# A four-layer attention network on one core: first keys and queries of the two split attentions made in other stages, and the last part of the network as one chunked stage

## What is computed

```python
x = x + _L0_xattn_ref(_layernorm(x), ctx_512, ...)
x = x + _L0_ffn_ref(_layernorm(x), ...)
...
x = x + _L2_ffn_ref(_layernorm(x), ...)
x = x + _L3_xattn_ref(_layernorm(x), ctx_512, ...)
x = x + _L3_ffn_ref(_layernorm(x), ...)

def fp4_quant_dequant(x):
    scale = jnp.maximum(jnp.max(jnp.abs(xb), -1, keepdims=True) / 6.0, 1e-12)
    idx = jnp.searchsorted(_MID, jnp.abs(xb / scale))
    return _GRID[idx] * jnp.sign(xb / scale) * scale
h = silu(fp4_linear(x, w_gate)) * fp4_linear(x, w_up)
return fp4_linear(h, w_down)
```

## Time and profile before

| | |
|---|---|
| median of 3 runs | 4032.26 us (4030.01 to 4044.68) |
| the profiled execution | 4038.64 us, span 4036.9 us |
| PE busy | 3242.3 us (80%) |
| DVE busy | 2389.7 us (59%) |
| ACT busy | 1805.8 us (45%) |
| POOL busy | 1094.5 us (27%) |
| mean granted TensorE clock | 0.905 of full speed |
| DMA | 89.94 MB, mean 22 GB/s |

### The profile page before, as it was taken

The page is one execution under the profiler, slowest core; times in us unless marked ns, Lnnn a source line. Parts: engine busy times, 40 slices in busy tenths (PEclk is TensorE's granted clock), DMA queues, the critical chain, the costliest instruction groups (busy, mean ns, idle before and its releaser), DMA issues. The chain is left out here.

```text
span 4036.9 us, 81036 instructions
## 1 busy us (share of the span) xinstructions
PE 3242.3 (80%) x33476; PEld 1634.2 (40%) x33476; DVE 2389.7 (59%) x3851; ACT 1805.8 (45%) x2194; POOL 1094.5 (27%) x767
## 2 busy tenths in 40 slices
PE   7985999999588827999999999977876799999821
PEld 5661333332266513444444444444542233333311
DVE  4554788878456454555555555433435688688676
ACT  2321677676333223444444444432211477677611
POOL 1002112110233253655565656631001111111000
PEclk9995999999799867999999999988877799899965
DMA  0003111110000030000000000001202211111000
GB/s 26 2 12 69 44 32 33 34 38 11 17 22 2 1 76 6 10 10 2 10 10 10 2 10 2 2 1 33 59 17 50 50 33 39 34 41 27 2 6 11
DMA packets 69858, 89.94 MB, mean 22 GB/s; under 512 B 37582, under 2 KB 50427, under 8 KB 69499
## 3 DMA queue, kind: packets, MB, share of 16 engines
q1 hardware_dynamic: 65642, 78.37, 8.6%
q10 hardware_dynamic: 3856, 6.47, 0.9%
HBM read 34.17 MB, written 4.33 MB: 10 GB/s over the span
## 5 line engine op out<-in xcount | busy, mean ns | idle before, releaser
L1970 DVE TENSOR_REDUCE mx<-ps 128x2 f32<-128x802 f32 (+1 forms) x1372 | 1028.2, 778 | 292.5 <-PE ps L1836 267.5
L1904 ACT ACTIVATE probs<-ps 128x1024 f32<-128x1024 f32 (+1 forms) x832 | 832.9, 1024 | 257.1 <-PE ps L1822 248.3
L2282 DVE TENSOR_REDUCE mx<-ps 128x3 f32<-128x1203 f32 (+1 forms) x352 | 483.1, 1373 | 476.7 <-PE ps L2178 476.7
L2330 POOL TENSOR_TENSOR sums<-sums,probs 128x2048 f32<-128x2048 f32 x128 | 579.1, 4524 | 143.7 <-ACT probs L2257 129.0
L1836 PE MATMUL ps<-kt,qs 48*128 48x401 bf16 x2048 | 472.4, 355 | 115.2 <-DVE mx L1970 79.0
L2257 ACT ACTIVATE probs<-ps 128x1024 f32<-128x1024 f32 x384 | 372.2, 1021 | 358.0 <-PE ps L2156 357.9
L1854 PE MATMUL ps<-probs,v_cur 128*9 128x256 f32 x6656 | 530.0, 391 | 0.4 <-ACT probs L1904 0.4
L2178 PE MATMUL ps<-kt,qt 32*128 32x401 f32 x2048 | 339.8, 556 | 46.4 <-DVE mx L2282 40.8
L1822 PE MATMUL ps<-qs,kt 50*128 50x256 bf16 (+1 forms) x3328 | 346.3, 281 | 1.8 <-ACT probs L1904 1.4
L2011 POOL CAST max_pieces<-negm 128x8 bf16<-128x8 f32 x64 | 12.1, 189 | 1122.2 <-DVE negm L1975 1122.2
L1836 PEld LDWEIGHTS ps<-kt,qs 48*128 48x128 bf16 x2048 | 134.6, 95 | 331.8 <-DVE mx L1970 255.6
(11 more groups left out here) (402 smaller groups left out, 4268.0 us busy)
## 6 DMA issues: line engine op xcount, KB each, us to landing
kt<-k SPq DMA_DIRECT2D x776, 50.0 KB
ctx_s<-in_ctx_t SPq DMA_DIRECT2D x16, 400.2 KB, 4.6
ctx_s<-ctx_norm_t SPq DMA_DIRECT2D x16, 400.2 KB, 5.5
qs<-q ACTq DMA_DIRECT2D x24, 192.0 KB
ctx_norm_t<-ctx_norm_t SPq DMA_DIRECT2D x8, 400.2 KB
ctx_a<-in_ctx_t SPq DMA_DIRECT2D x8, 400.2 KB
ctx_b<-in_ctx_t SPq DMA_DIRECT2D x8, 400.2 KB
ctx_tok<-in_ctx SPq DMA_DIRECT2D x8, 384.0 KB
```

Of the source, the lines that this page charges most:

```text
L1904: act.activation(pr[0:m, u % 3, :], pair[0:m].rearrange("p a n -> p (a n)"), ACT.Exp, scale=scale).then_inc(s_free, 1)
L1970: dve.tensor_reduce(mx[:, n % 2, i0:i0 + count], src, AX_X, ALU.max).then_inc(freed(step), 1)
L2282: dve.tensor_reduce(mx[:, n % 2, 3 * i0:3 * i0 + count], rbanks[:, 0:count, 0:CH], AX_X, ALU.max).then_inc(ring_free, 1)
L2330: pool.tensor_tensor(o, o, p, ALU.add).then_inc(added, 1)
```

## The change

Two things, in one edit.

**First keys and queries ready.** `SplitTiles` holds the buffers of `split_cross` outside of it, with `kt` as two tensors, `kt0` and `kt1`. `FirstKeys` makes the keys of batch 0 in earlier stages: in `layer0` inside `normalized` (loads, projection, drains) and in the new `first_queries` (pieces on POOL), which also holds the former `int4_lora` and projects and splits all queries of layer 0 on DVE; the 24 sends of keys and queries and five of the seven weight loads go into `self_heads`, whose SP issued nothing in `layer0`. For `layer3` the loads are in the `normalized` of the layer 2 FFN, and projection, drains, pieces and sends in `experts`. Layer 3's queries stay in `split_cross`: the first 512 are split by DVE and sent half by SP and half by ACT, the other 1536 are split by POOL after the first `cut` and sent by SP.

**One last stage.** `finish` replaces everything from the transpose of y to the store. It works in four chunks through PE, ACT, DVE and POOL, quantizes with a shorter chain, treats the three weights as one array of 1120 columns (loaded in layer 3's `normalized`, after a `clear`), and stores each chunk when it is done.

```diff
+class FirstKeys:
...
+    def fetch(self, sp):
+        for dst, src in self.loads:
+            sp.dma_start(dst, src).then_inc(self.ctx_in, 16)
...
+    def project(self, pe, k):
+
+        pe.wait_ge(self.ones_set, 1)
+        pe.wait_ge(self.ctx_in, 32)
+        for c, (lo, hi) in enumerate(CHUNKS):
+            pe.matmul(k.ps[:, 4 + c, 0:hi - lo], self.wk[0:R, :], self.tiles.ctx_s[0:R, 0, lo:hi], start=True,
+                      stop=True).then_inc(self.filled, 1)
...
+    def send(self, sp):
+        for i, (dst, src) in enumerate(self.tiles.key_sends()):
+            sp.wait_ge(self.cut, (1, 3, 4)[sorted(KPIECE)[i // 2]])
+            sp.dma_start(dst, src).then_inc(self.sent, 16)
+        sp.wait_ge(self.sent, 16 * 2 * PIECES)
...
+def first_queries(nc, k, keys, tiles, xt, wcq, bcq, y, w, at, b):
...
+        @block.tensor
+        def _(pe):
+            for c in range(4):
+                pe.matmul(k.ps[:, 4 + c, :], wcq, xt[:, cols4(c)], start=True, stop=True).then_inc(filled, 1)
+            pe.matmul(k.ps[:, 1, 0:C], at, b, start=True, stop=True).then_inc(lora, 1)
...
+            qp = tiles.qp
+            dve.wait_ge(drained, 4)
+            dve.tensor_copy(qp[0][:], qf).then_inc(cut, 1)
+            dve.wait_ge(cut, 1)
+            dve.tensor_tensor(qf, qf, qp[0][:], ALU.subtract).then_inc(cut, 1)
+            dve.wait_ge(cut, 2)
+            dve.tensor_copy(qp[1][:], qf).then_inc(cut, 1)
+            dve.wait_ge(cut, 3)
+            dve.tensor_tensor(qp[2][:], qf, qp[1][:], ALU.subtract).then_inc(cut, 1)
+
+        @block.gpsimd
+        def _(pool):
+            keys.pieces(pool)
...
-    slots = [(-80.0, ("qproj", 0))] + [(-70.0 + c, ("qproj", c)) for c in range(1, 4)]
-    steps = [(-90.0, ("ctx", 0)), (-90.0, ("ctx", 1)), (-89.0, ("ones",)), (-74.0, ("qsplit", 0)), (-73.9, ("qsend", 0)),
-             (-42.4, ("qsplit", 1)), (-42.3, ("qsend", 1))]
+    slots, steps = [], [(-90.0, ("ones",)), (-89.0, ("ctx", 1))]
+    if not ready:
+        slots += [(-80.0, ("qproj", 0))] + [(-71.0 + c, ("qproj", c)) for c in range(1, 4)]
+        steps += [(-69.9, ("qsplit", 0)), (-69.8, ("qsend", 0)), (3, ("qsplit", 1)), (25, ("qsend", 1))]
     for b in range(B):
...
-        slots += [(at - 22.5 + c, ("kproj", b, c)) for c in range(4)]
-        steps += [(at - 17 + 2.4 * i, ("ksplit", b, i)) for i in range(4)]
...
+        if b >= 1:
+            slots += [(at - 22.5 + c, ("kproj", b, c)) for c in range(4)]
+            steps += [(at - 17 + 2.4 * i, ("ksplit", b, i)) for i in range(4)]
...
+def fp4_round(dve, x, n, scales, a, e, step, base):
...
+    dve.tensor_reduce(rs, x, AX_X, ALU.max, apply_absolute_value=True).then_inc(step, 1)
...
+    dve.tensor_scalar(sc, rs, 1.0 / 6.0, 1e-12, ALU.mult, ALU.max).then_inc(step, 1)
...
+    dve.reciprocal(rs, sc).then_inc(step, 1)
...
+    dve.tensor_scalar(rs, rs, FRACTION, None, ALU.mult).then_inc(step, 1)
...
+    dve.tensor_tensor(by16(an), x, wide(rs), ALU.mult).then_inc(step, 1)
...
+    dve.tensor_scalar(en.bitcast(I32), an.bitcast(I32), POWER, None, ALU.bitwise_and).then_inc(step, 1)
...
+    dve.tensor_scalar(en, en, 1.0, TWO_BITS, ALU.max, ALU.mult).then_inc(step, 1)
...
+    dve.tensor_tensor(an, an, en, ALU.add).then_inc(step, 1)
...
+    dve.tensor_tensor(an, an, en, ALU.subtract).then_inc(step, 1)
+
+
+def fp4_scaled(pool, x, n, scales, a):
+    wide = scales[:, 0, 0:n].rearrange("p (n a) -> p n a", a=1).broadcast_to([P, n, 16])
+    return pool.tensor_tensor(x, by16(a[:, 0:16 * n]), wide, ALU.mult)
...
+    plan = [("y", 0), ("wo", 0), ("y", 1), ("wo", 1), ("w", 0), ("n", 0), ("gu", 0), ("y", 2), ("wo", 2), ("n", 1),
+            ("gu", 1), ("y", 3), ("wo", 3), ("h", 0), ("down", 0), ("n", 2), ("gu", 2), ("h", 1), ("down", 1), ("n", 3),
+            ("gu", 3), ("h", 2), ("down", 2), ("h", 3), ("down", 3)]
...
+        def _(sp):
+            for c in range(4):
+                sp.wait_ge(final, c + 1)
+                sp.dma_start(out[:, tiles4(c), :], k.x[:, tiles4(c), :]).then_inc(stored, 16)
...
+            def gate(c):
+                for t in range(NC * c, NC * c + NC):
+                    pool.wait_ge(silu_done, t + 1)
+                    pool.wait_ge(up_done, t + 1)
+                    pool.tensor_tensor(h[:, t, :], silu[:, t % 2, :], up[:, t % 2, :], ALU.mult).then_inc(gated, 1)
...
-def experts(nc, k, hid_t, w2, w):
+def experts(nc, k, hid_t, w2, w, keys):
...
             for t in range(NT):
+                if t == 2:
+                    keys.project(pe, k)
+                    pe.wait_ge(keys.drained, 4)
```

More of the change, by code:

```diff
@@ L191, in _ @@
         def _(sp):
+            if keys is not None:
+                keys.fetch(sp)
             if src_dram is not None:
@@ L217, in _ @@
         def _(pool):
+            if keys is not None:
+                keys.set_ones(pool)
             for c in range(4):
@@ L2001, in _ @@
                     split_queries(pool, 1)
-                elif kind == "ksplit" and step[1] >= 1:
+                elif kind == "ksplit":
                     split_keys(pool, step[1], step[2])
@@ new lines, in hidden, with last @@
+            def hidden(c):
+                dve.wait_ge(gated, NC * c + NC)
+                fp4("h", c)
+            def last(c):
+                dve.wait_ge(down_done, c + 1)
+                dve.tensor_tensor(k.x[:, tiles4(c), :], bank4(k.ps[:, 7, :]), k.x[:, tiles4(c), :], ALU.add).then_inc(final, 1)
+            fp4("w", 0)
+            add(0)
+            add(1)
+            norm(0)
+            norm(1)
+            add(2)
+            hidden(0)
+            norm(2)
+            add(3)
+            hidden(1)
@@ L2613, in experts, with _ @@
         block = ctx.enter_context(nc.Block())
+        @block.sync
+        def _(sp):
+            keys.send(sp)
+        @block.scalar
+        def _(act):
+            keys.drain(act, k)
+        @block.gpsimd
+        def _(pool):
+            keys.pieces(pool)
         @block.tensor
```

525 lines of the change are left out of this document (327 added, 198 removed).

## The result

The changed kernel takes **3915.36 us** (median of 4 runs, 3909.63 to 3935.75) against 4038.47 for the kernel before (4 runs, 4030.01 to 4045.15): ratio 0.9705, 95% interval 0.9662 to 0.9749. The profiled execution took 3919.61, its span is 3917.8 against 4036.9. So 123 us went between the medians, 119.1 between the spans. The forecast was 158, so its value, 3874, is missed by 41 us; its range, 3837 to 3924, holds the time.

The account below looks back on a forecast made before the run. The two long loops are near a real bound; three chains, 392 us or 9.7% of the span, have no engine near full. +9 - 48 + 3 + 2 - 34 - 90 = -158, hence 3874 us; range 3837 to 3924.

Parts of the forecast that it names:

- The three chains: Starts of layer 0's and layer 3's split attentions and the last stage: no engine near full; 392 us, 9.7% of the span.
- The stalls: Last stage: DVE waits for the output projection's third chunk, 5 to 12 us, and before h's last chunk, 6 to 13.
- The half-clock case: Last stage with PE at the lower clock throughout: 135 us against 106 at full clock; as a rival, chance 0.15.
- The rival by which all of POOL's time goes on top of DVE's: Last stage: POOL's 30 us add to DVE's 80, about 140 us; kernel 3895 us; chance 0.13.
- I cost them at nothing: Layer 0's self attention: key and query sends there cost 0; if not covered, 5.6 MB at 91 GB/s, 61 us.
- DVE's cuts in their own stage: Layer 0's second stage: with projections and DVE's cuts of 2048 query columns, 14.7 us for 8.5, +6.2.
- 12 sends are 2.46 MB, 27 us at 91 GB/s: Layer 2's experts: time of the key sends, plus 2 us to land; 38.6 us against 36.8 + 1.5.
- the third rival: Experts' 12 key sends end 13 us late, 10 over forecast, and the queries' backlog costs 4 more: 3888 us; chance 0.06.
- the +3: Layer 2's experts: forecast growth of the stage in us, with +6 at 78 GB/s and +13 if sends begin after POOL's last piece.
- 4 units, +6 us: Layer 3's loop: the fourth group's maxima queue behind twelve query sends, 26 us at 91 GB/s; bounds 0 and +10.
- The first two stages: Layer 0: +2.5 us for key loads in the first stage, +6.2 in the second; +9, bounds +5 and +16.
- the clearing: Layer 3's `clear`, one block more: +2 us, 1 to 3.

Follow-up runs that it names:

- e_ctx: The changed kernel, but SP issues the context of batch 1 ahead of the four sends of rows of ones, in both attentions: 3913.08 us.
- e_gate: The changed kernel, but DVE does the last stage's sixteen gatings in place of POOL, reading the up projection from PSUM, without ACT's copy: 3921.20 us.
- e_paced: The changed kernel, but each of layer 0's 24 key and query sends waits until the one before has landed: 3912.88 us.
- The added products: The changed kernel, but PE does eight 512-column products that nobody reads while DVE cuts layer 0's queries: 3921.65 us.

## Why the prediction's range held, and which of its terms were wrong

**The three chains: right.** The first scores came 47.0 and 49.1 us after the starts, for 42 and 48. The 5 us in layer 0 are one number, the context's landing: 9.7 for 4.6; with it out of the way (e_ctx) the first scores come 36.8 us after the start, 5 better than forecast. POOL's split of batch 1 waited for no key sends. The last stage took 115.2 for 124; DVE was busy 86.4, that is 80 and 6.4 more, for 7 forecast. That is luck in part: POOL cost DVE 4.5 us by its gatings (e_gate) and 5.3 by its scalings (read from the timeline), 9.8 in all, so DVE's own steps were 3.4 under the forecast's 80. The stalls were 5.7 and 5.9, at the places named. PE's clock was neither of the two cases: 0.71, and the time lay between them. (The half-clock case was added up wrongly: its terms, 80, 12, 13 and 19, give 124 and not 135.) The rival by which all of POOL's time goes on top of DVE's fell: POOL was busy 40 us, and DVE paid 10. That the two take turns where they meet did not fall. The Trainium skill, "SBUF — State Buffer", section "SBUF: two separate sides", says that steps of DVE and GpSimd that need the shared ports hold them in turn, for a whole instruction; the trace agrees, with DVE's step of 0.34 us held for POOL's 2.6. What the rival had wrong is how much of POOL's time meets such a step.

**"I cost them at nothing" (the sends in the self attention): wrong, +17.7.** I had looked for engines that wait for those sends, and there are none. But PE's own code comes through the same DMA engines: 4.1 to 7.7 us of pauses, and the clock at 0.50 behind them. This is 8.2 of the 17.7 us, and pacing takes it away (e_paced). The other 9.4 lie at the start and the end of the stage, where PE ran at half clock for part of the time. I had priced DVE's cuts in their own stage (+6.2) and not what 12.7 us of idle PE may do to the next one. The added products took the loss at the end away; at the start it came in four profiles of eight, so what sets it stays open. The Trainium skill, "Runtime: NRT & Kernel Launch", section "Instruction fetch mechanics", says that an engine's sequencer fetches its code in blocks of 16 KiB through a DMA queue of its own, mostly hidden; the trace agrees on the block (16 KB packets), and shows a case in which it is not hidden.

**"12 sends are 2.46 MB, 27 us at 91 GB/s" (the experts): wrong, +15.6 for +3.** The step that failed is the rate. 91 GB/s was taken from a row in which nearly half the traffic was small key sends; the new sends moved 60 GB/s, so that the 2.46 MB took some 41 us (3014.6 to 3055.3) for the 27 forecast. That is the outcome of the third rival, "the sends are not hidden", to which I had given 0.06, and almost its number (13 us late was said, 12.6 were measured). The number is luck: the 13 stood for sends that begin only after POOL's last piece, but they were issued from 3013.2 on, 8 us before it. And the +3 was too much for its own terms, which give 38.6 us for 36.8.

**"4 units, +6 us" (the query burst): wrong in size, +22.1.** Place, cause and the waiting instruction were as forecast, and the small send did not overtake the large ones. The backlog was mis-sized by the same rate: from the first issue at 3160.9 until PE had the maxima at 3202.2 it was 41 us, not 26, and PE's wait 18.6 for 6. The rest is the clock at 0.50 behind the wait.

**The first two stages, +12.5 for +9.** The four query projections took 6.43 us for the 3.7 that I had taken from the experts' rows; there a record of 512 columns took 0.80 us for the experts' 0.46, though the granted clock reads 1.00 over both.

The losses, 55 us for 9 forecast, are 46 more than I had, and the first stages and the two starts another 9; 9 in the last stage, 7 in stages not touched and 1 in the clearing went the other way, and the total came out 39 short. The forecast was held by its range because this took in the rivals' prices, not because its terms were right.

## What to carry to other kernels

A transfer that nobody waits for is not free: it queues ahead of the next small transfer on its engines, ahead of the loads of the stage behind, and, as the pauses say, ahead of the engines' own code. Give big sends a pace (one after the other, or with units of work between them), put whatever somebody waits for in front of them, and take their rate from a row that has such sends alone. A stage that leaves PE idle for 10 us may be paid for in the next one, where its clock can be low: here 0 to 7 us at the next stage's start. And before two profiles are compared by the length of a stage, compare them step by step: that shows where the time went, which two lengths don't.
